# A scan of 256 chunks and its read-out on one core: products ordered by array division, the bias carried in a running sum, output banks copied by ScalarE

## The reference

```
Z1      = xk @ W1 + b1
grad    = gradient of the layer-norm loss of Z1 against xv - xk
Attn1   = tril(xq @ xk.T)
b1_bar  = b1 - tril(eta) @ grad
Z1_bar  = xq @ W1 - (eta * Attn1) @ grad + b1_bar
W1      = W1 - (last_eta * xk).T @ grad
b1      = b1 - sum(last_eta * grad)
out     = xq + layernorm(Z1_bar)
```

## Time and profile before

| | us |
|---|---|
| median of three runs (lowest, highest) | 6555.11 (6519.12, 6576.57) |
| the profiled execution | 6570.32 |
| its span, first to last instruction | 6568.5 |
| mean granted TensorE clock over the span | 0.908 of full speed |
| stretch of the scan and its read-out, 1731 to 4668 us | 2937 |

### The profile page before, as it was taken

One profiled execution on the slowest core, in us unless ns is written; L12 is line 12 of the kernel. 1 busy time (PEld: TensorE's weight loads), 2 busy tenths in 40 slices (PEclk: granted clock), 3 DMA queues, 4 the chain that ended last, 5 costly groups with the idle time before them and its releaser, 6 DMA issues. The chain is left out here.

```text
span 6568.5 us, 136994 instructions
## 1 busy us (share of the span) xinstructions
PE 5831.2 (89%) x39482; PEld 4065.8 (62%) x39482; DVE 4090.7 (62%) x14673; ACT 2173.4 (33%) x6003; POOL 2140.4 (33%) x3398
## 2 busy tenths in 40 slices
PE   1799999999598898999988988998789999599999
PEld 0344444444377777777777777777666666367777
DVE  5566666665467666766777677667656666544444
ACT  0111111111244444444444444444333333233433
POOL 0244444444233333333333333333211222122222
PEclk9899999999588888888888889888899999799999
DMA  6233333333334343433444344334332221112221
GB/s 234 83 114 128 128 120 123 126 122 119 117 102 108 105 107 105 109 104 106 107 109 107 106 107 115 104 101 111 85 119 83 83 83 65 64 71 89 92 94 66
DMA packets 823380, 692.97 MB, mean 105 GB/s; under 512 B 357400, under 2 KB 758176, under 8 KB 811840
## 3 DMA queue, kind: packets, MB, share of 16 engines
q1 hardware_dynamic: 732480, 542.55, 27.7%
q10 hardware_dynamic: 90240, 142.75, 5.8%
HBM read 402.97 MB, written 282.20 MB: 104 GB/s over the span
## 5 line engine op out<-in xcount | busy, mean ns | idle before, releaser
L1390 PE MATMUL proj_ps<-proj_w_sb,proj_h 128*128 128x512 f32 x3072 | 1345.5, 596 | 0.0
L1390 PEld LDWEIGHTS proj_ps<-proj_w_sb,proj_h 128*128 128x128 f32 x3072 | 577.2, 190 | 743.4 <-issue 716.6
L2170 PE MATMUL scan_ps_y<-scan_o_t,proj_wo_sb 128*128 128x128 f32 x4096 | 666.6, 313 | 1.5 <-DVE scan_y L1963 0.9
L1312 DVE SCALAR_TENSOR_TENSOR proj_lin<-proj_ps,proj_rstd,proj_wbias_sb 128x512 f32<-128x512 f32 x384 | 284.4, 747 | 536.1 <-PE proj_ps L1390 535.1
L2170 PEld LDWEIGHTS scan_ps_y<-scan_o_t,proj_wo_sb 128*128 128x128 f32 x4096 | 565.3, 214 | 64.4 <-issue 23.0
L1736 POOL TENSOR_TENSOR scan_stored<-scan_core,scan_rate 128x128 f32<-128x128 f32 x512 | 332.7, 650 | 665.0 <-DVE scan_core L1947 665.0
L1785 ACT ACTIVATE scan_square<-scan_ps_z 128x64 f32<-128x64 f32 x1024 | 219.8, 220 | 946.6 <-PE scan_ps_z L2090 946.6
L1926 DVE TENSOR_TENSOR scan_zg<-scan_ps_z,scan_gain 128x128 f32<-128x128 f32 x512 | 146.0, 285 | 582.5 <-ACT scan_square L1785 578.7
L1729 POOL TENSOR_TENSOR scan_rate<-scan_rstd,scan_record 128x2 f32<-128x2 f32 x512 | 100.8, 197 | 1147.3 <-DVE scan_rstd L1929 1147.2
L2102 PE MATMUL scan_ps_w<-scan_step,scan_record 64*128 64x128 f32 x4088 | 438.4, 343 | 4.3 <-DVE scan_step L1952 4.3
L2161 PE MATMUL scan_ps_out<-scan_q_t,scan_k_t 64*128 64x128 f32 x2048 | 201.6, 350 | 209.1 <-DVE scan_zn L2016 209.1
(11 more groups left out here) (288 smaller groups left out, 12256.4 us busy)
## 6 DMA issues: line engine op xcount, KB each, us to landing
scan_record<-records SPq DMA_DIRECT2D x1032, 98.0 KB
records<-proj_rec ACTq DMA_DIRECT2D x128, 784.0 KB, 3.6
scan_k_in<-records SPq DMA_DIRECT2D x266, 128.0 KB, 2.8
spectra<-fourier_spec SPq DMA_DIRECT2D x16, 2112.0 KB, 6.4
fourier_spec<-spectra SPq DMA_DIRECT2D x16, 2112.0 KB, 8.1
stats_x<-x SPq DMA_DIRECT2D x16, 2048.0 KB, 8.2
proj_h<-x SPq DMA_DIRECT2D x32, 1024.0 KB, 7.4
queries<-proj_q ACTq DMA_DIRECT2D x128, 256.0 KB, 3.7
```

Source lines behind the costliest of these rows:

```text
L1312: v.scalar_tensor_tensor(lin[q][:, n], ps[q][n][:], rstd[k][:, j:j + 1], T.wbias[:, n], ALU.mult, ALU.add).then_inc(lin_sb.sem, 1)
L1390: last = pe.matmul(ps[j % 2][n][:], h[k][:, ct, j * P:(j + 1) * P], T.w[:, n, ct], start=ct == 0, stop=ct == CT - 1)
L2170: done = pe.matmul(ps_y[:, n], T.wo[:, ct, n * P:(n + 1) * P], o_t[:, ct], start=ct == 0, stop=ct == CT - 1)
```

## The change

- The bias's start value goes into `b_sum` once, at the start (in the row of each head's first token), and `b_sum` now carries the factor of the last token: GpSimd multiplies `core` by rate and factor into `b_step`, adds it, and only then makes `stored`. The index product is gone.
- The head product becomes four products of 32 columns (128x32), in the strips of the state products behind it.
- The bias product of the read-out reads 64 rows of `b_sb` (rows that no snapshot fills are zero) instead of 17.
- ScalarE copies ps_out to `zo` in SBUF and squares that; VectorE makes `zn` from `zo` in one instruction. `tile_weights` waits for `zo`, no longer for `zn`.
- The order on TensorE: query transposes move from the end of the even chunk into the odd one, behind project_k(0); weighted products move behind project_k(1); key transposes move behind the last part of the projection; the first part of the projection follows update(0).
- ScalarE's copies of the transposed keys move from the odd chunk to the next even one, ahead of `normed`.
- Five small loads at the start of the stage are gone.

```diff
@@ gpsimd, gradients
-                v.tensor_tensor(rate_pair[g][:], rate[g][:].unsqueeze(2).broadcast_to([P, PB, 2]),
-                                pair_last[:].unsqueeze(1).broadcast_to([P, PB, 2]), ALU.mult).then_inc(rate_sb[g].sem, 1)
+                v.tensor_tensor(rate_last[g][:], rate[g][:].unsqueeze(2).broadcast_to([P, PB, 3]),
+                                pair_last[:].unsqueeze(1).broadcast_to([P, PB, 3]), ALU.mult).then_inc(rate_sb[g].sem, 1)
+                pool.wait_ge(rate_sb[g].sem, rate_sb[g].at(s, 2))
+                pool.wait_ge(b_sum_sb[g].sem, b_sum_sb[g].at(s, 0))
+                pool.wait_ge(core_sb[g].sem, core_sb[g].at(s, 1))
+                v.tensor_tensor(b_step[g][:], core[g][:], rate_last[g][:, :, 2:3].broadcast_to([P, PB, HD]),
+                                ALU.mult).then_inc(b_step_sb[g].sem, 1)
...
+                v.tensor_tensor(b_sum[g][(c + 1) % RING][:], b_step[g][:], b_sum[g][c % RING][:], ALU.add
+                                ).then_inc(b_sum_sb[g].sem, 1)
                 pool.wait_ge(grad_gone[g][c % 2].sem, grad_gone[g][c % 2].at(at.v * 8 + at.p * 4 + c // 2, 0))
-                pool.wait_ge(core_sb[g].sem, core_sb[g].at(s, 1))
                 v.tensor_tensor(stored[g][c % 2][:], core[g][:], rate[g][:].unsqueeze(2).broadcast_to([P, PB, HD]),
                                 ALU.mult).then_inc(stored_sb[g].sem, 1)
...
-                v.tensor_tensor(b_sum[g][(c + 1) % RING][:], stored[g][c % 2][:], b_sum[g][c % RING][:], ALU.add
-                                ).then_inc(b_sum_sb[g].sem, 1)
@@ scalar
             def squares(tile):
                 t, b, sc, _ = tile
-                act.wait_ge(hsq_sb.sem, hsq_sb.at(t, 0))
+
+                act.wait_ge(zn_sb.sem, zn_sb.at(t, 0))
                 for n in range(2):
                     act.wait_ge(out_ps.sem, out_ps.at(t, n + 1))
-                    a.activation(zsq[:].rearrange("p (a n) e -> p a n e", n=2)[:, :, n], ps_out[n][:, :, 0:HD], ACT.Square
-                                 ).then_inc(zsq_sb.sem, 1)
+                    a.copy(zo[:].rearrange("p (a n) e -> p a n e", n=2)[:, :, n], ps_out[n][:, :, 0:HD]).then_inc(zo_sb.sem, 1)
+                act.wait_ge(hsq_sb.sem, hsq_sb.at(t, 0))
+                act.wait_ge(zo_sb.sem, zo_sb.at(t, 2))
+                a.activation(zsq[:], zo[:], ACT.Square).then_inc(zsq_sb.sem, 1)
...
+                if not at.odd and (scan or at.slot == 0) and not (isinstance(at.s, int) and at.s == 0):
+
+                    keys_out(at.v * 8 + at.slot + B - 1, at.p if at.c == 0 else 1 - at.p, (at.c // 2 - 1) % B)
...
-                    if scan:
-                        keys_out(at.v * 8 + at.slot + B, 1 - at.p, at.c // 2)
@@ vector
-            for q in range(2):
-                for n in range(2):
-                    row, mean = b_sb[q][64 * n:64 * n + 1], mb_row[64 * n:64 * n + 1]
-                    steps.then(dve, v.tensor_reduce(mean, row, AX.X, ALU.add))
-                    steps.then(dve, v.scalar_tensor_tensor(row, mean.unsqueeze(2).broadcast_to([1, HP, HD]), -1.0 / HD, row, ALU.mult, ALU.add))
...
+            for q in range(2):
+                steps.then(dve, v.memset(b_sb[q][:], 0.0))
...
+            dve.wait_ge(first_ps, 1)
+            for g in range(GR):
+                for b in range(PB):
+                    steps.then(dve, v.tensor_copy(b_sum[g][0][:, b], ps_z[0][:, 0:HD]))
+            dve.sem_inc(first_sb, 1)
...
-                for n in range(2):
-                    done = v.tensor_tensor(zn[:].rearrange("p (a n) e -> p a n e", n=2)[:, :, n], ps_out[n][:, :, 0:HD],
-                                           hrstd[:].rearrange("p (a n) -> p a n", n=2)[:, :, n:n + 1].broadcast_to([P, HP, HD]), ALU.mult)
-                done.then_inc(zn_sb.sem, 1)
+                v.tensor_tensor(zn[:], zo[:], hrstd[:].unsqueeze(2).broadcast_to([P, NH, HD]), ALU.mult).then_inc(zn_sb.sem, 1)
@@ tensor
-                pe.matmul(ps_z[g][:, 0:F], ind[:], b0[:].rearrange("p b e -> p (b e)"), start=True, stop=False, skip_group_check=True)
                 pe.wait_ge(b_sum_sb[g].sem, b_sum_sb[g].at(s, 0))
-                pe.matmul(ps_z[g][:, 0:F], heads[:], b_sum[g][at.c % RING][:].rearrange("p b e -> p (b e)"), start=False, stop=False,
-                          skip_group_check=True)
+                for a in range(HP):
+                    pe.matmul(ps_z[g][32 * a:32 * a + 32, 0:F], heads[:, 32 * a:32 * a + 32],
+                              b_sum[g][at.c % RING][:].rearrange("p b e -> p (b e)"), start=True, stop=False, skip_group_check=True)
...
-                    rows = slice(64 * n, 64 * n + CS + 1)
+                    rows = slice(64 * n, 64 * n + 64)
                     pe.matmul(out[n], ones[rows], b_sb[q][rows], start=True, stop=False, skip_group_check=True)
...
-                pe.wait_ge(zn_sb.sem, zn_sb.at(t, 0))
+                pe.wait_ge(zo_sb.sem, zo_sb.at(t, 0))
@@ tensor, body
                 if scan:
                     project_k(0, at)
                 if at.odd:
+                    if kq:
+                        tile_query_turn(kq, proj)
                     if proj:
                         tile_project(proj, 1)
                 elif out:
                     tile_bias_and_state(out)
-                if scan and not (isinstance(at.s, int) and at.s == 0):
+                if update_last:
                     update(1, before)
                 if at.odd:
                     if proj:
                         tile_project(proj, 2)
-                else:
-                    if proj:
-                        tile_outputs_turn(proj)
-                    if out:
-                        tile_weighted(out)
+                elif proj:
+                    tile_outputs_turn(proj)
                 if scan:
                     project_k(1, at)
                 if at.odd:
                     if kq:
                         tile_weights(kq)
+                elif out:
+                    tile_weighted(out)
+                if scan:
+                    update(0, at)
+                if at.odd:
+                    if proj:
+                        tile_project(proj, 3)
                     if scan:
                         if kq:
                             pe.wait_ge(q_t_sb.sem, q_t_sb.at(kq[0], 1))
                         turn_keys(at.v * 8 + at.slot + B)
                 elif proj:
                     tile_project(proj, 0)
-                if scan:
-                    update(0, at)
-                if at.odd:
-                    if proj:
-                        tile_project(proj, 3)
-                elif kq:
-                    tile_query_turn(kq, proj)
```

More of the change, by code:

```diff
@@ L1551, in scan_and_read @@
         out_ps = one("out_ps", 2)
-        zsq_sb = one("zsq_sb", 2)
+        zo_sb = one("zo_sb", 2)
+        zsq_sb = one("zsq_sb")
         hsq_sb = one("hsq_sb")
@@ L1608, in _ @@
         def _(sp):
-            for dst, src in ((gain8, d["gain_rows"]), (heads, d["heads"]), (ind, d["ind"]), (ends, d["ends"]), (w0_in, d["w0"]),
+            for dst, src in ((gain8, d["gain_rows"]), (heads, d["heads"]), (first, d["first"]), (w0_in, d["w0"]),
                              (b0_in, d["b0"]), (pair_in, d["pairs"]), (masks_in, d["masks"]), (read_eps, d["eps"])):
@@ L1885, in _ @@
             steps.then(dve, v.tensor_scalar(last[:], last[:], 0.0, 1.0 / 8, ALU.max, ALU.mult))
-            steps.then(dve, v.tensor_scalar(pair_last[:], pair_in[:], last[:], None, ALU.mult))
+            steps.then(dve, v.tensor_scalar(pair_last[:, 0:2], pair_in[:], last[:], None, ALU.mult))
+            steps.then(dve, v.tensor_copy(pair_last[:, 2:3], last[:]))
             steps.then(dve, v.memset(eps[:], HD * 1e-6))
@@ L2065, in _ @@
             made.then_inc(start_ps, 1)
+            pe.matmul(ps_z[0][:, 0:HD], first[:], b0[:], start=True, stop=True).then_inc(first_ps, 1)
+            pe.wait_ge(first_sb, 1)
             def turn_keys(count):
@@ L2179, in body @@
                 before = Place(at.v, at.p, at.c - 1) if at.c else Place(at.v - 1 + at.p, 1 - at.p, 7)
+                update_last = scan and not (isinstance(at.s, int) and at.s == 0)
                 if scan:
@@ L2459, in shape_constants @@
         "heads": heads.T @ heads,
-        "ind": heads,
-        "ends": np.stack([np.arange(P) % 64 == 0, np.arange(P) % 64 != 0], 1),
+        "first": heads * np.tile(np.repeat(np.eye(CS)[0], 2), NH // 2),
         "tok_inv": np.tile(1.0 / np.arange(1, CS + 1, dtype=np.float32), NH),
```

46 lines of the change are left out of this document (20 added, 26 removed).

## The result

The changed kernel takes 6308.15 us (median of 4 runs, 6305.94 to 6322.01) against 6565.84 for the kernel before in the same session: ratio 0.9624, 95% interval [0.9572, 0.9676]. The forecast was 6255, in a range of 6070 to 6430. The profiled execution took 6306.89 us, its span is 6304.9.

A forecast was written before the change was run, and what follows sets the result against it. SyncE's queue was taken as the longest ring at the full clock, 19.3 us a pair, plus 1.5 for the clock: 20.8 us. Saving 2.5 x 123 = 305 us gave 6255 us, range 6070 to 6430.

The forecast's parts named there:

- forecast case: The predicted main outcome: 20.2 to 21.7 us a pair, 6180 to 6360 us, chance 0.65.
- rival D: Strips of the head product don't overlap: TensorE 17.9 us, 170 to 205 us saved, about 6370; chance 0.07.
- TensorE's turn: TensorE's own work per pair of chunks, predicted to fall by 2.9 us to 15.1 us at the full clock.
- VectorE's ring: VectorE's time per pair without its two waits: 17.4 us, plus 0.5 for blocking by GpSimd, 17.9 us.
- Setup: Start of the stage: VectorE loses nine short operations, gains four copies; -4 to +2 us once, taken as 0.
- SyncE's issues: SyncE's DMA queue per pair, measured at 19.9 us, taken at 19.3 us and as the longest ring.
- The clock: Cost of TensorE's half-clock stretches in the stage: 1.94 us a pair before, taken as 1.5 us after.
- Rival C: TensorE, with less work, waits more and stays at 1.2 GHz: slower, for example +185 us, 6740; chance 0.06.
- The scan_zn wait: TensorE's wait for scan_zn at the key-query products, 208 us or 1.6 us a pair, predicted to go.
- Divisions: Fewer changes of TensorE's array form, 25 to 14 a pair; scan projections save 2.3 us, bias 0.2.
- Order: Key transposes moved save two changeovers; weighted products moved give VectorE group 1's products 1.8 us earlier.
- GpSimd blocking: GpSimd's added product per gradient makes VectorE stand still: 0.5 us a pair taken, bounds 0 to 2.

The follow-up runs named there:

- after: The changed kernel itself, without further edits, against the kernel before: 6308.2 us, ratio 0.9624.
- e5: Changed kernel with the loads of group 1's records issued by ScalarE instead of SyncE: 6271.2 us.
- e6: Changed kernel with group 1's record loads on ScalarE and four unused filling products ahead of the even chunks' bias product: 6047.5 us.
- e1: Changed kernel with four unused filling products on TensorE ahead of the bias product of every even chunk: 6264.9 us.
- e8: Changed kernel with the output banks squared by ScalarE and read by VectorE into zn, as before the change: 6227.0 us.
- e4: Changed kernel with one whole head product and an 8-row index product back, new order kept: 6393.4 us.
- e7: Changed kernel with TensorE's and ScalarE's order of the kernel before, the rest of the change kept: 6501.7 us.
- e11: Kernel before the change with group 1's record loads on ScalarE and two unused filling products ahead of the bias product: 6480.1 us.
- e10: e6 with one GpSimd product fewer per gradient, the last token's factor put into head and bias weights instead: 6010.1 us.

## Why the prediction was right

The total was: 258 us are saved by the medians where 305 were forecast, and 6308 lies within the forecast case's own 6180 to 6360. The split was not, and it took luck for the total to come out.

*Right.* Head and state products 0.25 us apart and 0.58 us a projection (0.2 and 0.6 said), so rival D is out. TensorE's turn 14.9 us (15.1). VectorE's ring was put at 17.9 us: full-clock pairs have a median of 18.4 us in after, e5 and e6, and the pair shown took 17.94. The waits for scan_zn and for the root went. The wait before the bias product grew, to 3.02 us in the pair shown (3 said) and 2.0 a pair over the stage. SyncE waited 0.8 us a pair (under 1.5).

*Setup: missed, though small.* It was taken as 0, between -4 and +2 us. The first bias product came 8 us earlier; SyncE's first load of keys already starts at 1705.2 us instead of 1713.1.

*SyncE's issues: mis-sized.* Taken at 19.3 us a pair, "near the measured end" of 19.9; they measure (2590.0 - 99.6)/123 = 20.2 in the changed kernel and 20.7 when never held up (e1). The 19.9 was low itself: it divides by 128 pairs a stretch that doesn't hold so many. By the 123 distances that the pair is counted with, give (2864.1 - 391.1)/123 = 20.1. Nothing in the rows of before gave a reason to go under the measured value.

*The clock: the step that failed in kind.* The sum takes the longest ring and adds 1.5 us of clock, two things that overlap. The clock by itself would hold the pair at 20.7 (e5), SyncE by itself at 20.7 (e1), both together at 21.06. By the prediction's own reckoning the full-clock pair was to be 19.3 us and the clock 1.5; they are 18.42 and 21.06 - 18.42 = 2.64. One is too high by 0.9 us and the other too low by 1.1, so the forecast of 20.8 is close by luck. The clock's own price, with SyncE out of the way, is 1.8 us (e5 to e6). The half-clock time grew from 7.05 to 7.54 us a pair, where the prediction let the clock's price fall from 1.94 to 1.5. Rival C's mechanism was real, at a small share of its price. The Trainium skill's rule that speaks for it ("TensorE: Matmul & The Clock Gate", HAM oscillation — how this bites in real kernels: waits between bursts of products bring the clock down, and a loop that runs its products without these waits keeps it up) agrees in kind with the windows above and with e6.

*The scan_zn wait: right that it goes, wrong that 1.6 us a pair go with it.* TensorE doesn't set the full-clock pair, so it waits about as long wherever it waits. The time came back before the bias product (254.5 us at the two places before, 247.9 after); moved back (e8), it cost less clock.

*Divisions: right in TensorE's turn.* The sum, set by SyncE, gave the 2.3 us of work removed no price of their own; they were worth 0.5 us a pair (e4). *Order: underrated.* It was costed at 0.4 us of changeovers and an unpriced relief of VectorE; taking it back costs 1.5 us (e7), the most of the parts tried. *GpSimd blocking:* 0.5 us taken. VectorE's operations that got longer or shorter make 0.2 us a pair in all, and 0.2 came of taking the product away (e10).

Still open: why scan_ovar is long (means of 0.15 us in e11, 0.37 in e10 without the added product, 0.28 in e8 with it), so that neither the product nor zn's source explains it alone.

## What to carry to other kernels

When a profile shows two limits within a few per cent of each other, remove both in one experiment before judging either: here each alone gave 0.3 us of a 21 us pair and both gave 2.1 (in the kernel before, the same two edits gave only 0.7). Add up what an in-order DMA queue issues per turn and treat a queue that never waits as an engine. When one engine is relieved and another sets the turn, ask where the relieved one will now stand idle: with TensorE the same idle time cost 7.5 us a pair at the half clock at one place and 3.7 at another, for a reason that stays open.

## What the runs showed of the hardware

- Products that compute nothing shortened the kernel by 224 us (e6 against e5); the stage's granted clock rose from 0.82 to 0.98.
- Behind four products of 32 columns (eight instructions) the state products start 0.25 us after them at the full clock and 0.43 us at the half clock; behind an 8-row product and a whole head product together it was 0.83 and 1.44 us (e4).
- The part behind the last bias product, alike in every kernel here but for the last tiles' read-out, took 1898 to 1931 us. A difference of 20 us between two kernels can be that.
